# Five reorderings in the queues of a 16-chunk Mamba2, SwiGLU and quantized-FFN kernel

## The reference, cut to what matters

```
x = x + 0.5 * ffn(layernorm(x))
n = layernorm(x)
h = n + mamba2(rmsnorm(n))          # in-projection, conv of 4 taps, SSD scan in chunks of 128, gate, out-projection
x = x + h + silu(h2 @ gate.T) * (h2 @ up.T) @ down.T      # h2 = rmsnorm(h), inner size 1792
x = x + 0.5 * ffn(layernorm(x))
```

## Time and profile before

| what | value |
|---|---|
| three runs, median (lowest to highest) | 774.79 us (774.35 to 776.3) |
| the profiled execution, its own time | 775.83 us |
| its span | 774.1 us |
| mean granted TensorE clock | 0.998 |
| TensorE busy | 755.7 us, 98% |
| DVE busy | 628.5 us, 81% |
| ACT busy | 446.0 us, 58% |
| GpSimd busy | 337.5 us, 44% |
| chain that ended last | PE 67%, DVE 20%, ACT 5%, issue 4%, DMA 2%, POOL 2% |

### The profile page before, as it was taken

The page is one execution under the profiler, slowest core; times in us unless marked ns, Lnnn a source line. Parts: engine busy times, 40 slices in busy tenths (PEclk is TensorE's granted clock), DMA queues, the critical chain, the costliest instruction groups (busy, mean ns, idle before and its releaser), DMA issues.

```text
span 774.1 us, 10655 instructions
## 1 busy us (share of the span) xinstructions
PE 755.7 (98%) x3470; PEld 352.5 (46%) x3470; DVE 628.5 (81%) x1230; ACT 446.0 (58%) x881; POOL 337.5 (44%) x392
## 2 busy tenths in 40 slices
PE   8899999999999989999999999999999999999998
PEld 3344554454544444444443444444444444444443
DVE  7798878878878979878799878878878878667994
ACT  4777767766776666643645556456456456444441
POOL 5631534663442379765413343243243243224573
PEclk9999999999999999999999999999999999999999
DMA  8833534553321211420520733733733733444565
GB/s 294 203 67 61 153 75 88 103 110 69 69 55 28 42 37 41 114 54 1 132 45 14 177 69 68 163 69 68 164 69 68 162 70 66 80 73 78 114 163 136
DMA packets 95414, 71.86 MB, mean 93 GB/s; under 512 B 65232, under 2 KB 72400, under 8 KB 95360
## 3 DMA queue, kind: packets, MB, share of 16 engines
q0 software_dynamic: 17280, 31.46, 22.7%
q1 hardware_dynamic: 77600, 39.66, 19.4%
q10 hardware_dynamic: 480, 0.07, 0.1%
HBM read 20.32 MB, written 4.19 MB: 32 GB/s over the span
## 4 chain that ended last, share of the span: by engine, by line
PE 67%; DVE 20%; ACT 5%; issue 4%; DMA 2%; POOL 2%; ACTq 0%; POOLq 0%; DVEq 0%
PE PS L1957 55%; PE PS L2080 4%; DVE raw L1449 2%; DVE S L1817 2%; DVE xds L1819 1%; PE PS L2088 1%; DVE st L1288 1%; PE PS L2180 1%; DVE stage L1449 1%; PE PS L2053 1%; DMA x_t<-hb 1%; PE PS L2062 1%; DVE state L1431 1%; PE PS L2070 1%; PE PS L2045 1%
## 5 line engine op out<-in xcount | busy, mean ns | idle before, releaser
L712 POOL DMA_DIRECT2D xs<-x x59 | 50.9, 863 | 152.8 <-ACT x L1159 138.0
L1957 PE MATMUL PS<-h,w_in 128*128 128x512 f16 x480 | 108.7, 379 | 0.0
L1957 PE MATMUL PS<-h,x_t 128*128 128x512 f16 x408 | 94.0, 379 | 0.0
L1957 PEld LDWEIGHTS PS<-h,w_in 128*128 128x128 f16 x480 | 47.0, 98 | 64.9 <-issue 14.8
L1957 PE MATMUL PS<-n_T,stage 128*128 128x512 f16 x288 | 71.5, 379 | 0.6 <-ACT x L1159 0.6
L1159 ACT ACTIVATE x<-PS,d_d 128x512 f32<-128x512 f32 x59 | 40.2, 682 | 41.2 <-PE PS L1957 41.2
L1957 PEld LDWEIGHTS PS<-h,x_t 128*128 128x128 f16 x408 | 39.5, 98 | 48.5 <-issue 2.0
L521 POOL TENSOR_TENSOR r<-mv,mhalf 128x1 f32<-128x1 f32 (+1 forms) x32 | 29.1, 908 | 70.4 <-DVE mv L1292 56.5
L712 POOL DMA_DIRECT2D xs<-n x29 | 25.2, 869 | 72.6 <-ACT n L1159 62.1
L1957 PE MATMUL PS<-pre,stage 128*128 128x512 f16 x192 | 49.3, 379 | 0.6 <-ACT x L1159 0.6
L1129 ACT ACTIVATE xds<-tm,dgh 128x512 f32<-128x512 f32 x24 | 17.3, 722 | 52.1 <-DVE tm L1886 52.1
(11 more groups left out here) (314 smaller groups left out, 1819.8 us busy)
## 6 DMA issues: line engine op xcount, KB each, us to landing
xs<-x POOLq DMA_DIRECT2D x75, 256.0 KB, 3.3
xs<-n POOLq DMA_DIRECT2D x29, 256.0 KB, 3.3
x_t<-x_in SPq DMA_DIRECT2D x16, 256.0 KB, 3.0
x_t<-hb POOLq DMA_DIRECT2D x16, 256.0 KB, 3.9
out<-x_t SPq DMA_DIRECT2D x16, 256.0 KB, 2.3
raw_gu<-gate_t SPq DMA_DIRECT2D x7, 512.0 KB, 4.4
raw_gu<-up_t SPq DMA_DIRECT2D x7, 512.0 KB, 6.5
raw_d<-down_t SPq DMA_DIRECT2D x7, 512.0 KB, 7.5
```

The source lines that it names most:

```text
L712: po.dma_start(chunk_of(xs, c), d_tmps[d % 3], accum_op=ALU.add).then_inc(s_acc[d % 3], 16)
L1957: ins = pe.matmul(out_, lhs(a, b, k), rhs(a, b, k), start=first and n == 0, stop=last and n == len(todo) - 1)
```

## The change

It moves work inside the queues of GpSimd, ACT and DVE; no instruction is added or taken away.

- GpSimd: `ln0(5)` before `ln1_chain(3)`.
- DVE, scan: `gate_mid` also holds for step 7. `scales(0)` and `descale(0)` of step 10 stand behind `slot_b` and no longer ahead of `cut_decay`.
- ACT and DVE, MLP: part 0 of `st_a(p+1)` stands ahead of the first eviction only in unit m = 3, and else behind `tanh_s(m, 0)`, as the other parts do; `st_g(p+1)` likewise keeps its place in unit 3 and else stands just ahead of DVE's `st_a(p+1)`.
- Closing: ACT's `c_hi(3)` goes between the two last `hi_s`, DVE's `c_lo(3)` ahead of `tail(4)` and `tail(5)`.

```diff
@@ gpsimd
             po.sem_inc(e_const, 1)
+            ln0(5, 1)
             ln1_chain(3, 3)
-            ln0(5, 1)
             xb(5, 1)
@@ scalar, weight_work
-                    if n == 3 and part > 0:
+                    if n == 3 and (part > 0 or p > 1):
                         st_a(p + 1, part)
@@ scalar, unit
-                if p + 1 < NP and n == 3:
+                if m == 3:
                     st_a(p + 1, 0)
                 evict(ds[0])
                 tanh_s(m, 0)
@@ scalar, end
             hi_s(NU - 1, 0)
+            c_hi(NC - 1, NC - 1)
             hi_s(NU - 1, 1)
-            for c in range(NC - 1, NCH):
+            for c in range(NC, NCH):
                 c_hi(c, c % NC)
@@ vector, step
-                gate_mid = (j == 2 and a < NCH) or (a >= NCH and c <= 3 * CH and j != 2)
+                gate_mid = (j == 2 and a < NCH) or (2 * CH - 1 <= c <= 3 * CH and j != 2)
@@
                     lo1(a, a % CH)
-                if c == 2 * CH + 2:
-                    scales(0)
-                    descale(0)
                 if j == 2 and i + 1 < NS:
                     cut_decay(i + 1, 0)
@@
                 if i + 1 < NS:
                     slot_b(i + 1, SLOTS[j][0])
+                    if c == 2 * CH + 2:
+                        scales(0)
+                        descale(0)
@@ vector, unit
-                if p + 1 < NP and n == 3:
+                if m == 3:
                     st_g(p + 1)
@@
                 if p + 1 < NP and n == 3:
+                    if m > 3:
+                        st_g(p + 1)
                     st_a(p + 1)
@@ vector, end
             c_lo(2, 2)
+            c_lo(3, 3)
             tail(4)
             tail(5)
-            c_lo(3, 3)
```

## The result

The changed kernel took 767.04 us, median of five runs (766.01 to 768.65), beside 774.79 for the kernel before (774.35 to 776.3, five runs of the same comparison): ratio 0.9896, 95% interval 0.9881 to 0.9912, 7.75 us less. The forecast was 767.0. In the kernel after, TensorE's lines are 3 higher and DVE's 1 to 3 higher than before.

The account below looks back on a forecast made before the run. TensorE, busy 98% of the span, was taken as the bound. Against the median, -1.6 - 0.4 - 1.4 - 3.0 - 1.2 = -7.6 gave 767.2 us, against the profiled execution 766.5; forecast 767.0, range 764.8 to 770.6.

Parts of the forecast that it names:

- Part 1: GpSimd's prologue, ln0(5) ahead of ln1_chain(3): first_f(5) starts 1.6 us earlier; -1.6 against the median, bounds -1.0 and -1.6.
- The in-projection can follow: Prologue: the in-projection moves earlier along with first_f(5), the cut of the first weights and DVE's half; within the -1.6.
- The clock: Prologue, from 38 us: a 1.2 GHz stretch costing 1.7 us goes; the median run is taken to have none.
- Part 2: Scan, gate_y(7) ahead of chunk 15's statistics: w(7) starts 1.0 us earlier, 0.4 arrives; -0.4, bounds 0 and -1.0.
- Part 3: Scan, scales(0) and descale(0) behind the slot: silu 1.8 us earlier, cut_a 1.36 earlier; -1.4, bounds -0.3 and -1.8.
- The bound of 0.3: Scan, scales(0) move: gain only 0.3 us if GpSimd's T sums catch the moved chain and DVE loses 1.1.
- Part 4: MLP, gate weights of pairs 3 to 6 behind the first eviction: four stops of 0.74 us go; -3.0.
- rival (e): MLP: gate weights of the next pair come late, TensorE waits at each pair's first product; slower, 777.2 us; chance 0.02.
- Part 5: Closing, c_hi(3) and c_lo(3) earlier: the stop at the fourth closing product goes; -1.2 us, bounds 0 and -1.2.
- (b): Prologue: the clock dip stays or moves elsewhere there, and the median run has it; 768.9 us, chance 0.12.
- (c): Scan's ACT-DVE chain gives back parts 2 and 3 (768.8 us), or MLP evictions still come late (770.2); 0.20 together.
- (d): Whole kernel: little happens, because waits of this kind come back one stage on; 772.5 to 777 us, chance 0.04.

Follow-up runs that it names:

- e1: Kernel before with only ln0(5) moved ahead of ln1_chain(3): 773.33 us against 774.49, ratio 0.9983.
- e2: Kernel before with only gate_y(7) and step 10's scales(0) and descale(0) moved: 772.47 us, ratio 0.9969.
- e3: Kernel before with only st_a's part 0 and st_g moved, in units 7, 11, 15 and 19: 771.83 us, ratio 0.9964.
- g1: Kernel before plus seven unused filler products in TensorE's idle times ahead of first_f(5): 774.67 us against 775.11, ratio 0.9995.
- e5: Changed kernel with gate_y(7) put back behind chunk 15's statistics: 767.79 us, ratio 0.991.
- e8: Changed kernel with DVE's gate weights (st_g) left at the old place behind u2, ACT's order kept as changed: 767.37 us, ratio 0.9906.
- f3: Changed kernel with scales(0) and descale(0) between the taps and the silu of step 10: 767.08 us, ratio 0.9894.
- e4: Kernel before with only c_hi(3) and c_lo(3) moved in the closing: 773.68 us, ratio 0.9989.
- e7: Changed kernel with one of GpSimd's four early T sums of step 10 moved to step 11: 768.38 us, ratio 0.9919.
- f1: Changed kernel with one of step 10's four T sums put ahead of rms2(10), in GpSimd's idle time: 766.97 us, ratio 0.9892.
- e6: Changed kernel with the st_a and st_g moves in all five pairs, unit 3 included: 769.71 us, ratio 0.9936.
- f2: Changed kernel with three of step 10's four T sums put ahead of rms2(10), in GpSimd's idle time: 769.19 us, ratio 0.9922.

## Why the prediction was right, point by point

**Sum.** Behind 200 us the table gives 6.58 us for parts 2 to 5, where the prediction had 0.4 + 1.4 + 3.0 + 1.2 = 6.0. The medians differ by 7.75, which leaves 1.2 for part 1, where it had 1.6; e1's median says 1.16, both to within a microsecond or so. Two terms were off by 0.4 or more, in opposite directions, so that the total is hit to 0.1 is in part luck; so are the last 0.2 of it, since the sum against the median was 767.2 and 767.0 leaned to the profiled execution with its dip, which the median run does not have.

**Part 1, 1.0 to 1.2 us and not 1.6.** What was said of first_f(5) is shown: in all nine profiled kernels with the swap it starts 1.55 us earlier against first_f(4), in the five without it, it doesn't. "The in-projection can follow" is the step that failed. From the start of first_f(5) to the in-projection it takes 3.97 us in the three profiled kernels without the swap and without the clock's dip (e2, e3, g1) and 4.14 to 4.92, median 4.50, in the nine with it. In five of these (e5 to e8, f3) the wait that took its place has a name, here in the waits of e5:

```profile
PE PS L1960 <- DMA h<-hn_p: 0.7, 1, 0.7
```

That is the last transpose DMA of the prologue, and the landings have it in all nine: the in-projection starts 0.35 us behind it, where it was 0.96 behind in the three without the swap. In the other four the idle time is under 0.2 us and the view of waits names no DMA for it. Counted from the transpose two before it (h<-n_p), which goes out at 30.48 in e5 and at 30.12 in e2, this one was sent 1.5 us earlier in e5 and landed 0.1 earlier; over the nine it was sent 0.7 to 1.7 earlier and landed 0.0 to 0.8 earlier, median 0.35. On the same count the in-projection starts at 11.88 without the swap and at 10.49 to 11.27, median 10.92, with it: that is 0.96 for part 1.

Why did it land late? `xb(5)`, the accumulating DMA of GpSimd, waits for `hi0(5)` and so moved with it. In e2, without the swap, it went out behind the transpose in front of the last one, in e5 ahead of it (timelines of GpSimd and SP, in order of time, first e2, then e5):

```profile
35.14 1.23 SPq L443 DMA_TRANSPOSE h<-h2n_p  x1
...
36.38 0.92 POOL L536 DMA_DIRECT2D x_t<-hb  x1 [1.14 <-ACT n L767]
```

```profile
34.79 0.92 POOL L536 DMA_DIRECT2D x_t<-hb  x1 [0.19 <-issue]
...
35.48 1.66 SPq L443 DMA_TRANSPOSE h<-h2n_p  x1
```

In all nine this transpose landed 1.04 to 1.08 us behind `xb(5)`, 4.1 to 5.0 after it was sent (3.4 to 3.6 in the five without the swap), and the last one 0.9 to 1.0 behind it; in the five without the swap it is the last one that landed 1.07 to 1.13 behind `xb(5)`. So the landing of `xb(5)` sets the pace, by nine traces that agree; no run moves `xb(5)` by itself, so this is not shown by an experiment. The prediction allowed for a late landing ("a late landing could cost some tenths"), put nothing into the sum for it, and did not ask what else moves with `hi0(5)`.

**The clock.** Right, and now shown: the median run of before has no dip. Of 54 runs of before for which the granted clock was recorded beside the experiments, 11 had a mean of 0.998, and their times are 775.8 to 776.6; the others' are 773.9 to 776.2. Together with e2 to e4 it is 13 of 74 without part 1 and without fillers (0.997 the lowest), and none of 36 with part 1 (after, e1, e5, e7, e8, f1, f3; of after four runs at 1.0 and one at 0.999), none of 12 with fillers. At 13 in 74, 36 runs without one would come by chance once in a thousand. e6 and f2 have part 1 too and are left out of the 36. That the same two idle times were in e2 and e3, whose first_f(5) took 3.70, shows that the idle times do not decide it; that they make it possible rests on the 0 of 36 against the 13 of 74. The Trainium skill (TensorE: Matmul & The Clock Gate, Part 1) has the clock reviewed on a period that the kernel does not start; this scatter agrees with it. e6 and f2, which add stops of 2.73 and 2.26 us later on, show 0.998 or less again in two and four of four runs. For e6 no trace shows where; in f2 the dip can be seen where it falls, in the stretch from 274 us behind the stop that ended at 272.7 (granted clock 0.61, the last column but two):

```profile
274.00:278.00 4.00, 4.00 (x13) 1.63 (x12) 3.13 (x8) 3.97 (x11) 2.80 (x3) 0.61 0.37 68
```

**Part 2, 0.8 us and not 0.4.** The local 1.0 was right (1.02). "The chain can only get earlier where DVE waits for TensorE" is the step that failed: it looked for DVE's own waits and found 0.41. That route gave 0.11. It missed that DVE was also held by a GpSimd instruction that itself waited for TensorE, which gave 0.68. e5 measured the term, 0.81.

**Part 3, 1.4 us as forecast (1.43), by another hand-over.** Both stops went as said (0.70 to none, 1.05 to 0.29), 1.62 in all at 273.0, and the scales ran at 0.17 each. But what was late next was not the factor and cut_a: it was GpSimd's block behind rms2(10), which hands back 0.19 at 284.2; e7, which shortened it, gained 1.17 there with the factor where it was, and f3 gave the factor early and gained nothing. The block moved with square(10), as the prediction said of it, so little was lost; naming ACT's queue as the limit was wrong and happened to give the right number, which is luck. The bound of 0.3, DVE held once per sum, was not reached, since the sums start behind the scales (274.40 against 273.46 for the last of the four).

**Part 4, 3.05 us at its four evictions for 3.0** (3.00 to 3.13 by the table, 3.34 with g1's scatter). Right in mechanism and size; e8 shows that ACT's order is all of it, and e6 that rival (e) is real in unit 3, where GpSimd's sums stretch DVE's instructions just before (L1825 takes 1.64 and L1831 1.75 us beside them, 0.7 without) and TensorE already waits 0.33 for the weights. Its price is 2.4 us there; in the other four pairs nothing was late.

**Part 5, 1.2 us for 1.2.** Right.

**Rivals.** (b) falls with the clock's rows. (c) did not occur: of parts 2 and 3 2.23 us are left at chunk 12 and stay, and part 4's evictions came in time. The hand-over that did occur, of part 1 to a DMA, was in no rival. (d) and (e) did not occur.

**No better version was found.** The three that aimed at the stop of 1.02 (e7, f1, f2) gained 1.2 or less where they aimed and handed it back by chunk 14 or lost it at the silu, but for 0.2 in f1. f1's time, 766.97, can't be told from 767.04, so whether these 0.2 are worth having is open.

## What to carry to other kernels

When one engine is 98% busy, compare two traces instruction by instruction on that engine: the difference of the starts, read as steps, prices each edit to under a tenth at its own place, where times scatter by one microsecond. Before you say what is late next behind a wait that goes, list every engine that feeds the next stop, the helper with long instructions as well as the one whose order you touched, and ask which of them hangs on the moved work. The same goes for DMAs: list those whose start hangs on what you moved, since one of them can get in front of the transfer that is waited for. An in-order move costs all instructions that it is moved past, not only those named in the diff: count them in the trace at their pitch.

## What the runs showed of the hardware that was not expected

- **GpSimd and DVE hold each other up for whole instructions, but not all of DVE's.** In the changed kernel the small L1401 took 1.39 us beside GpSimd's 1.27 at 267.25 (0.28 in the kernel before, with nothing beside it); in e5 and in the changed kernel L1376 ended 0.55 behind GpSimd's end. But f1's add at 266.72, which reads one operand from PSUM, took its 0.67 although GpSimd's sum (266.60, 1.21 us) lay over all of it, and the first tap, with both operands in SBUF, was the one stretched. The Trainium skill (SBUF — State Buffer, "SBUF: two separate sides") says that such a lock binds DVE operations with two SBUF inputs, against GpSimd operations that read SBUF, or in a two-port mode. The trace agrees: the add kept its 0.67, and three taps took 2.62 where they take 2.30 in the changed kernel.
- **The granted clock reads 1.00 where it has no record.** In the changed kernel and in e3, two 512-column products take 1.91 to 2.07 us, in place of 1.02 to 1.13, from 6 to 10 us, while the clock's column reads 1.00 there. But the trace's record of the granted clock begins only at 10.42 and 10.05 us in these two, and at 3.90 to 6.84 us in the other twelve, and the column counts a stretch without a record as full. So the 1.00 is no measurement there. The pace is that of the slower of the two levels (1.2 GHz) and is full from where the record begins. At 12 us these two executions stand 2.62 and 2.10 behind the kernel before, the others 0.07 to 0.77; with the 0.83 and 0.31 by which their first product was late taken off, the slow start cost 1.8 us in each, about as much as the dip.
- **The end of a wait is worth more than its idle figure.** The idle rows 0.86, 0.57 and 1.05 were worth 1.02, 0.74 to 0.77 and 1.12 to 1.22 us when they went, 0.07 to 0.20 more each; the prediction had reckoned with 0.17.
